# Two cross-attention layers: turning the probabilities on TensorE, or on VectorE with SBUF-to-SBUF transfers

## What is computed

```python
h = layer_norm(x)                                   # x: 512 tokens x 512
qh = (h @ wq + bq);  kh = (ctx @ wk + bk);  vh = (ctx @ wv + bv)   # ctx: 1024 x 512
kh, vh = kh with one row bias_k more, vh with one row bias_v more
logits = qh @ kh.T / sqrt(128)                      # 512 x 1025
weights = softmax(logits)
x = x + concat(weights @ vh) @ wo + bo
```

## Time and profile before

| | us |
|---|---|
| median of 3 runs | 3102.29 (3101.78 to 3104.33) |
| the profiled execution, its own time | 3101.0 |
| its span, first to last instruction | 3099.1 |
| PE busy | 2969.7 (96%) |
| DVE busy | 1857.3 (60%) |
| ACT busy | 1602.5 (52%) |
| POOL busy | 968.7 (31%) |
| mean granted TensorE clock | 0.979 |

### The profile page before, as it was taken

How to read it: one execution, slowest core, us unless ns; L and a number is a source line. 1 busy time by engine, 2 the same in 40 slices (tenths; PEclk the granted TensorE clock), 3 DMA queues, 4 the chain that set the end, 5 groups by cost and what they waited for, 6 DMA issues and landing times.

```text
span 3099.1 us, 59920 instructions
## 1 busy us (share of the span) xinstructions
PE 2969.7 (96%) x21520; PEld 2496.7 (81%) x21520; DVE 1857.3 (60%) x3167; ACT 1602.5 (52%) x2964; POOL 968.7 (31%) x645
## 2 busy tenths in 40 slices
PE   6999899999999999997979998999999999999979
PEld 4666688888978888896856666888899788889957
DVE  4999655555555555555159996555555555555551
ACT  3888444444445444443438883444444444444443
POOL 2000234333333433333410003433333343333333
PEclk8999999999999999998979999999999999999999
DMA  7100011110010111000460000111100011110012
GB/s 201 42 2 2 18 44 44 36 36 29 29 33 30 44 36 36 29 25 28 157 160 8 2 2 18 47 41 36 36 29 29 33 32 41 36 36 29 25 34 75
DMA packets 40326, 127.49 MB, mean 41 GB/s; under 512 B 4848, under 2 KB 18416, under 8 KB 33776
## 3 DMA queue, kind: packets, MB, share of 16 engines
q1 hardware_dynamic: 40176, 125.48, 13.2%
HBM read 118.64 MB, written 6.82 MB: 40 GB/s over the span
## 4 chain that ended last, share of the span: by engine, by line
issue 64%; POOL 25%; PE 7%; DVE 1%; DMA 1%; POOLq 1%; SPq 0%; ACT 0%; DVEq 0%; ACTq 0%
POOL wa L392 7%; POOL kT L392 5%; POOL v L392 4%; PE ps_m L799 3%; POOL cT L392 3%; PE ps_s L799 3%; POOL qT L392 3%; POOL wo L392 2%; POOL x_res L416 1%; DMA x_res<-in_x 1%; DMA scr_q<-parts 0%; DVE hT L1280 0%; DMA st_x<-in_xT 0%; POOL hT L392 0%; POOLq L438 0%
## 5 line engine op out<-in xcount | busy, mean ns | idle before, releaser
L1436 DVE TENSOR_TENSOR pT<-ps_t,pT 128x512 fp32r<-128x512 f32 x512 | 329.7, 685 | 262.4 <-ACT pT L528 262.4
L799 PE MATMUL ps_s<-kT,qT 128*128 128x512 f32 x1536 | 414.1, 405 | 0.0
L799 PE MATMUL ps_m<-pT,v 128*128 128x256 f32 x3072 | 399.4, 286 | 2.7 <-DVE pT L1436 2.7
L799 PE MATMUL ps_m<-wa,ctxT 128*128 128x256 f32 x3072 | 381.7, 282 | 2.3 <-DVE proj L1395 1.7
L799 PEld LDWEIGHTS ps_m<-wa,ctxT 128*128 128x128 f32 x3072 | 376.4, 189 | 9.2 <-DVE proj L1395 2.6
L799 PEld LDWEIGHTS ps_m<-pT,v 128*128 128x128 f32 x3072 | 376.1, 191 | 3.2 <-DVE pT L1436 3.2
L799 PE MATMUL ps_m<-ctxT,wa 128*128 128x512 f32 x1536 | 374.7, 396 | 0.0
L392 POOL TENSOR_TENSOR wa<-stg_qk,wa 128x1024 fp32r<-128x1024 f32 x80 | 192.4, 2406 | 553.8 <-ACT wa L528 553.8
L645 ACT ACTIVATE pext<-lb,nm 128x1 f32<-128x1 f32 x256 | 75.2, 294 | 557.2 <-DVE nm L1428 557.2
L799 PEld LDWEIGHTS ps_m<-ctxT,wa 128*128 128x128 f32 x1536 | 286.2, 188 | 67.6 <-issue 1.0
L1423 DVE TENSOR_REDUCE nmx<-ps_s 128x1 f32<-128x1024 f32 x256 | 311.7, 1218 | 39.3 <-PE ps_s L799 39.3
(11 more groups left out here) (115 smaller groups left out, 4127.4 us busy)
## 6 DMA issues: line engine op xcount, KB each, us to landing
stg_qk<-in_wqk SPq DMA_DIRECT2D x40, 1024.0 KB, 4.8
stg_o<-in_wo SPq DMA_DIRECT2D x48, 512.0 KB, 3.4
stg_v<-in_wv SPq DMA_DIRECT2D x32, 512.0 KB, 3.5
q_stack<-scr_q SPq DMA_DIRECT2D x48, 128.0 KB, 4.4
st_ctx<-in_ctxT SPq DMA_DIRECT2D x8, 512.0 KB, 6.4
mask<-in_mask SPq DMA_DIRECT2D x2, 2048.0 KB, 12.4
bv_row<-in_bv SPq DMA_DIRECT2D x32, 128.0 KB, 2.9
k_stack<-scr_k SPq DMA_DIRECT2D x24, 128.0 KB, 4.8
```

Source lines behind the costliest of these rows:

```text
L799: mm = nc.tensor.matmul(out, lhs(x, c), rhs(y, c), start=start and c == 0 and i == 0, stop=stop and c == n_tiles - 1 and i == 2)
L1436: nc.vector.tensor_tensor(part[1], ps_t[q][:].rearrange("p (s n) -> p s n", s=4), f32(part[0]), sub).then_inc(t_lo, 1)
```

## The change

For 14 of the 16 heads of a layer, the turn of the probabilities no longer goes through TensorE. VectorE turns each tile in 32x32 blocks inside the partitions (`blocks`, a `STREAM_TRANSPOSE` of 128x1024 from `p` to `pb`), and SP then moves the 16 blocks of partitions with 32 transfers of 32 partitions by 512 elements each from `pb` into `pT[1]`. The first 16 wait for `x_free` (the first half of the value product that reads the same buffer is done), the other 16 for the whole product. ACT copies the result into the high half `pT[0]` (`hi_moved`, four pieces of 128x1024) and POOL makes the low half in place in `pT[1]` (`lo_moved`, four pieces). The value product of a head comes a head later and is one product of 24 matmuls with 512 columns, where there were two of 24 with 256. The first head and the last head of each layer are still turned by PE.

With that, all of these move:

- the PSUM banks `ps_t` and `ps_m` become one ring of four (`RING1`), with tables of numbers of their own (`M_...`);
- Q and K projections get their high part straight from PSUM by ACT with the bias (`hi_column`, `Identity`), and their low part by DVE from the same bank (`lo_column`); before, DVE wrote `proj`, ACT copied it and POOL subtracted. V projections stay as they were;
- `cT` (the values' high and low parts) lies over the two `proj` buffers, for one head of 512 tokens;
- the staging buffers `stg_v` and `stg_o` become one, `stg_vo`;
- the loop runs over pairs 1 to 6 and pair 0 stands in front of it as straight code; `rows0` is loaded later, into `gb`.

The core of the diff:

```diff
-                    def turned(t):
-                        off = (t % 2) * P
...
+                    def blocks(t, x):
+
+                        lt = t % LT
+                        if lt == 0:
+                            for i in range(2):
+                                dve.wait_ge(moved_in[i], 256 * x + 16)
+                        dve.wait_ge(exp_done, T + t + 1)
+                        nc.vector.transpose(pb[:].rearrange("p a (s n) -> p s a n", s=ST)[:, :, :, lt * 32:(lt + 1) * 32],
+                                            p[t % 2][:].rearrange("p (s a n) -> p s a n", a=4, n=32))\
+                            .then_inc(pb_done, 1)
...
+                def move_turned(x, pv, m):
+
+                    sp.wait_ge(pb_done, LT * x + LT + 2)
+                    apart()
+                    for i in range(2):
+                        if i == 0:
+                            sp.wait_ge(x_free, pv + 1)
+                        else:
+                            sp.wait_ge(m_filled, m + 1)
+                        apart()
+                        for e in range(4):
+                            for j in range(4):
+                                a = (j + e) % 4
+                                sp.dma_start(f32(pT[1][32 * a:32 * a + 32, j, i * 512:(i + 1) * 512]),
+                                             pb[32 * j:32 * j + 32, a, i * 512:(i + 1) * 512]).then_inc(moved_in[i], 16)
...
+                    def lo_moved(x, qs):
+                        for q in qs:
+                            pool.wait_ge(moved_hi, 4 * x + q + 1)
+                            lo(pair_of_tiles(pT[1], q), f32(pair_of_tiles(pT[1], q)), pair_of_tiles(pT[0], q))\
+                                .then_inc(moved_lo, 1)
...
+                    def hi_column(n, kind, h, dst):
+
+                        act.wait_ge(m_filled, rt + n + 1)
+                        act.sem_inc(apart_act, 1)
+                        nc.scalar.activation(dst[0], bank1(n)[:], ACT.Identity, scale=1.0,
+                                             bias=cols[:, bass.ds(at_cols + kind * HEADS + h, 1)]).then_inc(col_hi, 1)
...
+                    def hi_moved(x, qs):
+                        for q in qs:
+                            act.wait_ge(moved_in[q // 2], 256 * (x + 1) + 16)
+                            copy(pair_of_tiles(pT[0], q), f32(pair_of_tiles(pT[1], q))).then_inc(moved_hi, 1)
```

The pair's order on PE after the change:

```diff
+                        scores(4)
+                        project_v(n + V2, 2)
+                        scores(5)
+                        project_v(n + V3, 3)
+                        scores(6)
+                        scores(7)
...
+                        values(n + PV0, 0, None if first else x - 1)
...
+                        project_q(n + Q0, 0)
...
+                        project_k(n + K0[0], 0, 0)
...
+                        extra_logits(n + EX0, 0)
+                        project_k(n + K0[1], 0, 1)
...
+                        output([n + o for o in OUT0], 0, 2 * pr, range(LT))
...
+                        scores(8)
+                        project_q(n + Q1, 1)
+                        scores(9)
+                        project_k(n + K1[0], 1, 0)
+                        scores(10)
...
+                        extra_logits(n + EX1, 1)
+                        scores(11)
+                        values(n + PV1, 1, x)
+                        project_k(n + K1[1], 1, 1)
+                        output([n + o for o in OUT1], 1, 2 * pr + 1, range(LT))
...
+                        project_v(n + V[0], 0)
+                        project_v(n + V[1], 1)
```

More of the change, by code:

```diff
@@ L1164, in _ @@
[L1164 to L1174 removed]
+                        pe.wait_ge(qk_lo, 2 * (b * QK_B + 2 + f) + 4)
@@ new lines, in _ @@
+                        for i in range(2):
+                            project_k(n + L_K0[i], 0, i)
+                    values(n + (L_PV0 if more else E_PV0), 0, x - 1)
+                    turned(n + (L_T0 if more else E_T0), 4)
+                    scores(6)
+                    turned(n + (L_T1 if more else E_T1), 5)
+                    pe.wait_ge(vo_lo, b * VO_B + 2 * f + 3)
+                    output(out0[0:2], 0, HEADS - 2, (0, 1))
+                    scores(7)
+                    turned(n + (L_T2 if more else E_T2), 6)
@@ L1236, in summed @@
                     if lt > 0:
[L1237 removed]
+                        dve.wait_ge(free, n + lt)
                         apart()
@@ new lines, in _ @@
+                    denominators(0)
+                    at_cols = at_this
+                    extra_value(n + (L_PV0 if more else E_PV0), 0, HEADS - 2)
+                    at_cols = at_next
+                    turned(n + (L_T0 if more else E_T0), 4, LT * 2)
+                    maxima(6)
+                    turned(n + (L_T1 if more else E_T1), 5, LT * 2)
+                    output(out0[0:2], 0, (0, 1))
+                    maxima(7)
+                    turned(n + (L_T2 if more else E_T2), 6, LT * 2)
```

978 lines of the change are left out of this document (478 added, 500 removed).

## The result

| | before | after |
|---|---|---|
| median of the runs | 3102.03 | 3382.03 |
| span of the profiled execution | 3099.1 | 3378.5 |
| PE busy | 2969.7 (96%) | 2915.3 (86%) |
| DVE, ACT, POOL busy | 1857.3, 1602.5, 968.7 | 1941.7, 1578.7, 1232.9 |
| mean granted TensorE clock | 0.979 | 0.931 |

The ratio is 1.090 (95% interval 1.0886 to 1.0913). I had forecast 3068 us, within 2975 to 3165: the sign was wrong and the measured time lies outside the range. The loss is 280 us.

A forecast was written before the change was run, and what follows sets the result against it. PE, busy all 66.0 us of a pair, bounds the kernel. Own work 59.0 plus waits 2.0 and 2.7 makes 63.7: 28 pairs gain 64 us, edges lose 30, so 3101.0 becomes 3067, median 3068, range 2975 to 3165.

The forecast's parts named there:

- What leaves PE: PE in a pair: turns and smaller value products go, own work falls 7.0 us to 59.0; 196 us over 28 pairs.
- The price of a transfer: SP's bursts: 0.445 us an issue, so 16 transfers land 9.1 us after their start, a whole head's 16.2.
- My own rule: Each 0.1 us more per transfer costs 1.6 us a pair on chain one and 3.2 through the odd head.
- break-even: The pair's gain is gone when it takes 1.2 us more, at 0.025 us more per transfer.
- The second rival: ACT's queue: transfers land later, copies delay exponentials and bank drains; 3141, or 3275 at 0.6 us; chance 0.17.
- This is covered: Odd head's transfers land at 24.7 us, before ACT asks at 25.3; next scores' second exponential stands right behind on ACT.
- Chain one: Even head: transfers, ACT's copies, then the K drain that the fourth output product needs; new wait of 2.0 us a pair.
- chain two: Odd head: exponentials through POOL's low part, which the output products wait for; new wait of 2.7 us a pair.
- The clock: PE's granted clock: 1.00 in the loop, 0.73 after waits of 5 us; waits of 2 to 3 should leave it.
- VectorE's lock: Two small two-input DVE operations could wait up to 2.4 us each beside POOL; held covered and priced at nothing.
- The edges: Layer starts, last pairs and first pairs: bare turns and moved V projections, 30 us lost over both batches.

The follow-up runs named there:

- e8: The change with 16 wide transfers a head, ACT's copies moved later, the extra key column on ACT, and V and last-pair K projections moved on PE: 3029.8 us.
- e14: The change with 28 of the 32 transfers a head, the other 4 left out of the computation: 3275.8 us.
- e1: The change with half the elements of each row moved per transfer, 32 KB instead of 64 KB: 3369.5 us.
- e7: The change with 16 partitions instead of 32 moved by each transfer: 3371.4 us.
- e6: The change with one transfer of 128 KB for each block, 16 a head, all behind the value product: 3298.1 us.
- e9: The kernel of e8 with the 32 narrow transfers a head put back: 3317.9 us.
- e2: The change with only 8 of the 16 transfers of each half head issued, the others left out of the computation: 3149.6 us.
- e10: The kernel of e8 with the extra key column made by VectorE at the start of the pair again: 3054.4 us.
- e12: The kernel of e8 with V projections and last-pair scores moved at the layer edges and POOL's bias-row addition held back: 2972.9 us, ratio 0.959 to the kernel before.
- e5: The change with the extra key column's high and low part made by ScalarE instead of VectorE: 3384.9 us.
- e4: The change with VectorE's two short two-input operations in a pair given one SBUF input, part of the computation left out: 3380.7 us.

## Why the prediction was wrong

- **What leaves PE: right.** The pair's own work was forecast at 59.0 us; e8 has 59.5 of PE busy at full clock, in pairs that mostly take 60.4 to 60.6.
- **The price of a transfer: wrong, and the largest error.** I took 0.445 us from a burst of six loads from DRAM, and had no row of a transfer inside SBUF. It was 0.63. My own rule (1.6 + 3.2 us a pair for each 0.1 us) turns the 0.185 that were missing into 8.9 us, so 63.7 becomes 72.6; 72.8 was measured, and e14's time fits the rule's slope. That the sum comes out so well is in part luck. The rule makes all 8.9 us waits of PE, on top of 4.7. The trace has waits of (194 + 74) / 28 = 9.6 us a pair; the other 4 are PE's own work, 0.5 longer than I had it, and its lower clock. And 0.445 was read too low even for those loads. The trace of before has, for twelve of another burst and for the last five of the six:

```profile
30.31 6.77 SPq L307 DMA_DIRECT2D k_stack<-scr_k  x12
...
44.21 2.33 SPq L307 DMA_DIRECT2D q_stack<-scr_q  x5
```

The twelve take 0.56 us each (one of them 1.7), so not every burst had 0.445. The last five start 0.47 us apart; 2.67 / 6 was lower because the first issue is shorter and no gap follows the last. With 0.47, my rule adds 1.3 us a pair, and the 1.2 us of the break-even were gone before the result came. The second rival named this place, a break-even at 0.025 us more, and 3275 at 0.60; it got a chance of 0.17. The sign hung on 6% of one number that no row of before shows in kind, and that deserved far more. With 0.63 the rule gives 3317; the 65 us from there to 3382 lie almost wholly at the edges. I also thought of the price as bytes over a rate (132 GB/s). e1, e7 and e6 show that bytes have no part in it.
- **"This is covered" of the odd head's transfers: the step that also failed.** I had the odd head's burst landing 24.7 us after the start of its value product and ACT asking at 25.3. It lands at 30.4, ACT stands ready for the copies at 29.7, and the exponential behind the copies is what PE waits for ahead of the next value product: the third wait, 74 us in all, where I had none. I had named that coupling, but I took the landing as covered and put nothing for it into the sum. And I followed the landing to the copies on ACT, but not to the buffer that the transfers read. `pb` is single, so burst and turns in blocks can't overlap. The loop was at 2 x 16.2 + 27.5 = 60 us with my prices, hidden under 63.7; with the real ones it is at 71.1 in e9 and just under the other chain in the change.
- **Chain one and chain two: mechanism and place right.** 2.99 to 4.4 measured against 2.0 in most pairs (the dearer issue), and 2.93 (e2 and the change) against 2.7.
- **The clock: wrongly dismissed.** I wrote that waits of 2 to 3 us should leave it. The wait of 2.93 us in e2 has six matmuls at half pace behind it (granted clock 0.50, the lower of its two levels, 1.2 GHz instead of 2.4), and so has one of 2.15 in e10; the wait of 2.26 in the change has none. The trace of before had such a case, at the start of layer 1:

```profile
397.88 1.72 PE L1021 MATMUL ps_t<-ident,p 128*128 128x128 f32 x8 [1.97 <-DVE pT L1436]
399.25 2.73 PE L799 MATMUL ps_s<-kT,qT 128*128 128x512 f32 x6
```

The turn steps 1.37 us instead of 0.80 and the scores 2.57 instead of 1.47; the granted clock of this stretch is 0.57. An equally long wait at 941.99 has scores at full clock behind it. All turns and products that left PE should have taken 28 x 7.0 = 196 us off its busy time; it fell by 54. The other 142 us are mostly the same work at a lower granted clock: in e12, where the waits are gone and the mean clock is 0.977, PE is busy for 2790.9, 17 more than 2969.7 - 196. So a wait of about 3 us costs more than 4 where the clock falls behind it.
- **VectorE's lock: right for the extra column in the change (e5), for a reason that doesn't last.** Once PE sets the pace it does cost time: e10's trace puts its 25 us down to the lock on the denominators. In the change the denominators take at most 1.4 us, and no run shows what that costs. Nor do the turns in blocks show any wait for GpSimd (1.22 to 1.25 us, all of them), as forecast.
- **The edges: 30 forecast, some 90 measured.** The start of a layer went up by 6.8 and 8.0 us instead of 1.1, since the V projections had also covered DVE's low part of the normed tokens. e12 points to the lock beside GpSimd's row addition as what held it: it holds the addition back, moves one V projection back as well, and the wait is gone. Which of the two took it away was not tried apart. The last pair of layer 1 went up by 20.3 us instead of 4.5, because I counted bare turns and never followed POOL's queue there.

## What to carry to other kernels

Moving work off the bounding engine gains what it frees only if every chain and every closed loop through a single buffer stays below the new, shorter period: write the loops down (who releases the buffer, what fills it, what empties it), since no reordering shortens them. When the sign of a forecast hangs on a few per cent of a price that no row shows in kind, look at every row that comes near it, say so, and measure that price alone first. Count transfers, not bytes: 16 transfers of 128 KB took half of the queue's time of 32 of 64 KB. And keep the cover of the edges: what fills a gap in the old order often fills two.

## What the runs showed of the hardware

- Transfers from SBUF to SBUF of 16 or 32 partitions, issued by SP in a burst, cost 0.63 us of issue each, with 32, 64 or 128 KB; single loads in the same loop show 0.34. The DMA engines were busy for 0.19 to 0.22 of a burst with 32 KB, 0.40 with 64 KB and 0.81 with 128 KB. The median from the start of an issue to its landing: 1.9 to 2.0 us for 32 KB, 2.0 for 64 KB, 2.4 for 128 KB. What the 0.63 us consist of, and whether a second issuing engine would share the burst, was not tried.
- A 128x1024 fp32 turn in 32x32 blocks on VectorE takes 1.24 us.
- A VectorE operation on 128x2 fp32 with a single SBUF input took 0.17 us with no GpSimd operation beside it and 2.05 on average in the loop, beside GpSimd operations of 2.4 us (e4). An addition on 128x4 with two SBUF inputs took 4.8 us in eight pairs of e10, beside two such operations in a row.
- After waits of PE of 2.9 us and more, the next six matmuls took 2.3 to 2.7 us instead of 1.4 in several places, and the same came after a wait of 2.15 (e10, granted clock 0.51) and of 1.97 (before, 0.57). After waits of 2.26 and 2.99 in the change they ran at full pace, so length alone doesn't tell; what decides between them stays open.
